# Decoder layer on one core: the gate and up products in plain fp32 on the weights as loaded, instead of three rounded products on split weights

## The reference

```python
def _L0_ffn_ref(x, w_gate, w_up, w_down):
    def _sparsify_2to4(h):
        B, S, I = h.shape
        g = h.reshape(B, S, I // 4, 4)
        a = jnp.abs(g)
        _, idx = jax.lax.top_k(a, 2)
        pos = jnp.arange(4)
        mask = (pos == idx[..., 0:1]) | (pos == idx[..., 1:2])
        return (g * mask.astype(g.dtype)).reshape(B, S, I)
    h = jax.nn.silu(jnp.einsum('bsh,hi->bsi', x, w_gate)) * jnp.einsum('bsh,hi->bsi', x, w_up)
    h_sparse = _sparsify_2to4(h)
    return jnp.einsum('bsi,ih->bsh', h_sparse, w_down)
...
x = x + _L0_attn_ref(_layernorm(x, axis=-1), ...)
x = x + _L0_xattn_ref(_layernorm(x, axis=-1), ctx_512, ...)
x = x + _L0_ffn_ref(_layernorm(x, axis=-1), L0_ffn_w_gate, L0_ffn_w_up, L0_ffn_w_down)
```

## Time and profile before

| | |
|---|---|
| time, median of 3 runs | 443.65 us (442.87 to 443.71) |
| time of the profiled execution | 448.27 us |
| its span | 446.5 us |
| PE busy | 394.7 us, 2912 matmuls |
| DVE busy | 286.2 us |
| ACT busy | 202.2 us |
| POOL busy | 159.9 us |
| mean granted clock of PE | 0.965 of 2.4 GHz |

### The profile page before, as it was taken

How to read it: one execution, slowest core, us unless ns; L and a number is a source line. 1 busy time by engine, 2 the same in 40 slices (tenths; PEclk the granted TensorE clock), 3 DMA queues, 4 the chain that set the end, 5 groups by cost and what they waited for, 6 DMA issues and landing times.

```text
span 446.5 us, 7877 instructions
## 1 busy us (share of the span) xinstructions
PE 394.7 (88%) x2912; PEld 320.3 (72%) x2912; DVE 286.2 (64%) x616; ACT 202.2 (45%) x524; POOL 159.9 (36%) x159
## 2 busy tenths in 40 slices
PE   4988899889899999869899999979899999577794
PEld 3767777667698777747698877857698877345783
DVE  3696931788769932748769961578769931344273
ACT  1422641477334741557444552287344551386230
POOL 4358730378310420356520340267520430155000
PEclk9996999999999999989999999999999999869698
DMA  7976300240001400240000510232000500210000
GB/s 239 373 253 206 95 25 23 73 119 19 2 0 54 143 23 25 72 124 12 2 1 7 166 25 1 70 112 51 0 1 0 167 24 24 84 36 1 1 0 23
DMA packets 34292, 29.93 MB, mean 67 GB/s; under 512 B 18512, under 2 KB 28880, under 8 KB 34000
## 3 DMA queue, kind: packets, MB, share of 16 engines
q1 hardware_dynamic: 34256, 29.44, 21.1%
HBM read 20.26 MB, written 5.24 MB: 57 GB/s over the span
## 4 chain that ended last, share of the span: by engine, by line
PE 64%; DVE 14%; DMA 7%; issue 5%; ACT 4%; SPq 3%; POOL 2%; POOLq 0%; DVEq 0%; ACTq 0%
PE ps L526 13%; PE ps L587 10%; PE ps L404 9%; PE ps L472 6%; PE ps L601 6%; DVE rope L728 4%; PE ps L435 4%; PE ps L512 3%; DMA q<-qx 3%; PE ps L490 3%; PE ps L412 2%; DMA prob<-in_masks 2%; POOL prob L934 2%; DVE total L759 2%; DVE mx L745 2%
## 5 line engine op out<-in xcount | busy, mean ns | idle before, releaser
L934 POOL TENSOR_TENSOR prob<-prob,inv 128x512 f32<-128x512 f32 x80 | 83.0, 1042 | 105.9 <-DVE inv L765 105.7
L404 PE MATMUL ps<-xnT,wqk_sb 128*128 128x256 f32 x320 | 79.1, 397 | 1.0 <-ACT xnT L989 0.7
L404 PEld LDWEIGHTS ps<-xnT,wqk_sb 128*128 128x128 f32 x320 | 61.5, 198 | 13.9 <-issue 4.9
L1026 ACT ACTIVATE prob<-ps,mx 128x128 f32<-128x128 f32 (+1 forms) x128 | 52.7, 431 | 13.7 <-DVE mx L743 11.6
L1036 ACT ACTIVATE pT<-ps 128x512 f32<-128x512 f32 x80 | 47.8, 601 | 18.6 <-PE ps L472 18.4
L728 DVE TENSOR_TENSOR rope<-ps,trig_sb 64x512 f32<-64x512 f32 x80 | 55.0, 688 | 1.1
L927 POOL TENSOR_TENSOR qs<-rope 128x512 f32<-128x512 f32 x32 | 40.9, 1278 | 37.6 <-DVE rope L728 37.6
L472 PE MATMUL ps<-ident_sb,prob 128*128 128x128 f32 x320 | 49.9, 281 | 4.5 <-POOL prob L934 4.2
L472 PEld LDWEIGHTS ps<-ident_sb,prob 128*128 128x128 f32 x320 | 37.7, 142 | 12.5 <-POOL prob L934 8.4
L743 DVE TENSOR_REDUCE mx<-ps 128x2 f32<-128x512 f32 (+1 forms) x48 | 33.1, 690 | 20.1 <-PE ps L454 19.7
L913 POOL TENSOR_TENSOR rstd<-vareps,power 128x1 f32<-128x1 f32 x24 | 13.1, 550 | 88.5 <-DVE vareps L707 88.3
(11 more groups left out here) (86 smaller groups left out, 677.7 us busy)
## 6 DMA issues: line engine op xcount, KB each, us to landing
k<-kx SPq DMA_DIRECT2D x32, 128.0 KB, 2.9
q<-qx SPq DMA_DIRECT2D x32, 128.0 KB, 2.6
vb<-v_sb SPq DMA_DIRECT2D x56, 64.0 KB, 2.1
wqk_sb<-in_wqk SPq DMA_DIRECT2D x4, 512.0 KB, 8.2
work<-in_wgu SPq DMA_DIRECT2D x4, 512.0 KB, 9.4
wo_sb<-in_wo SPq DMA_DIRECT2D x1, 2048.0 KB, 15.8
x_ln<-in_x SPq DMA_DIRECT2D x4, 256.0 KB, 2.8
x_res<-in_x SPq DMA_DIRECT2D x4, 256.0 KB, 3.0
```

What stands on the lines that cost most here:

```text
L404: mm = pe.matmul(o[:, half, :], wqk_sb[:, k, g, half, :], xnT[:, 0, k, :], start=(k == 0), stop=(k == KT - 1))
L934: pool.tensor_tensor(p, p, inv[:, i % ND, 0:g].unsqueeze(2).broadcast_to([P, g, 512 // g]), ALU.mult).then_inc(s_norm, 1)
L1026: ins = act.activation(prob[:, i % ND, h * k:(h + 1) * k], ps[:, BANK_S + i % 2, h * k:(h + 1) * k], ACT.Exp, bias=mx[:, i % ND, h:h + 1], ...
```

## The change

The weights stay as they are loaded, in one fp32 tensor `wgu_sb`, filled by one transfer that SP issues behind the value copies `v_blocks`, ahead of `wd_sb`. `round_weights` and `split_weights` are gone, with the waits on `s_wlo`. ACT copies the transposed residual once, in fp32, into `x3T`; DVE's subtraction is gone. `gate_up` makes four fp32 matmuls per bank in place of twelve rounded ones, 32 in place of 96 per batch. The split queries get two tensors of their own (`q2_hi`, `q2_lo`).

```diff
-        wgu_hi = sb("wgu_hi", [P, KT, 2, FC * 4, P], F32R)
-        wgu_lo = sb("wgu_lo", [P, KT, 2, FC * 4, P], F32R)
+        wgu_sb = sb("wgu_sb", [P, KT, 2, FC * 4, P])
...
-        x3_hi = sb("x3_hi", [P, KT, S], F32R)
-        x3_lo = sb("x3_lo", [P, KT, S], F32R)
-
-        q2p = [t[:].rearrange("p k s -> p (k s)").rearrange("p (t g n) -> p t g n", t=TT, g=HG)
-               for t in (x3_hi, x3_lo)]
+        x3T = sb("x3T", [P, KT, S])
+
+        q2p = [sb(f"q2_{part}", [P, TT, HG, P], F32R) for part in ("hi", "lo")]
...
                     wait_filled(sp, "down", b - 1)
-                else:
-                    sp.wait_ge(s_wlo, WCHUNKS)
...
-            for c in range(WCHUNKS // 2):
-                sp.dma_start(raw[:, 2 * c:2 * c + 2, :].rearrange("p c n -> p (c n)"),
-                             flat(wgu)[:, 2 * c * wcols:(2 * c + 2) * wcols]).then_inc(s_wraw[c], 16)
...
             v_blocks(None)
+            sp.dma_start(wgu_sb[:], wgu).then_inc(s_wgu, 16)
             sp.dma_start(wd_sb[:], wd).then_inc(s_wd, 16)
...
-                    by_hi = [(wp, x3_hi, k, m) for m in range(2) for k in range(KT) for wp in (wgu_hi, wgu_lo)]
-                    by_lo = [(wgu_hi, x3_lo, k, m) for m in range(2) for k in range(KT)]
-                    for n, (wp, xp, k, m) in enumerate(by_hi + by_lo):
-                        if xp is x3_lo and use == "gate00":
-                            wait_drained(pe, "ln3", b)
-
-                        mm = pe.matmul(half_banks(use, b)[:, m, :], wp[:, k, w, c * 4 + 2 * j + m, :],
-                                       xp[:, k, :], start=(n == 0), stop=(xp is x3_lo and k == KT - 1),
-                                       skip_group_check=True)
+                    for m in range(2):
+                        for k in range(KT):
+                            mm = pe.matmul(half_banks(use, b)[:, m, :], wgu_sb[:, k, w, c * 4 + 2 * j + m, :],
+                                           x3T[:, k, :], start=(k == 0), stop=(k == KT - 1))
                     mm.then_inc(filled(use, b), 1)
...
                 if b == 0:
-                    pe.wait_ge(s_wlo, WCHUNKS)
-                pe.wait_ge(s_x3hi, b + 1)
+                    pe.wait_ge(s_wgu, 16)
+                wait_drained(pe, "ln3", b)
...
-                dve.wait_ge(s_x3hi, b + 1)
-                dve.tensor_tensor(x3_lo[:], half_banks("ln3", b), x3_hi[:].bitcast(F32), ALU.subtract)\
-                   .then_inc(drained("ln3", b), 1)
...
-            def split_weights(c):
-
-                pool.wait_ge(s_whi, c + 1)
-                pool.tensor_tensor(lo_c[c], raw[:, c, :], hi_c[c].bitcast(F32), ALU.subtract)\
-                    .then_inc(s_wlo, 1)
...
-            def round_weights(c):
-
-                act.wait_ge(s_wraw[c // 2], 16)
-                act.activation(hi_c[c], raw[:, c, :], ACT.Copy).then_inc(s_whi, 1)
...
-                act.activation(x3_hi[:], half_banks("ln3", b), ACT.Copy).then_inc(s_x3hi, 1)
+                act.activation(x3T[:], half_banks("ln3", b), ACT.Copy).then_inc(drained("ln3", b), 1)
```

More of the change, by code:

```diff
@@ L47 @@
 XU = XU0 + XU1
-WCHUNKS = 8
-EARLY = 6
 UNITS = NQB + XU
@@ L125, in build @@
         rowmask_sb = sb("rowmask_sb", [P, HPT + 2])
-        wcols = KT * 2 * FC * 4 * P // WCHUNKS
         x_ln = sb("x_ln", [P, TT, D])
@@ L174, in build @@
         k4 = sb("k4", [P, HPT // 2, 2, HG, S], F32R)
-        raw = work[:].rearrange("p (c k) s -> p c (k s)", c=WCHUNKS)
         hidden = work[:, 0:4 * FC, :].rearrange("p (c j) s -> p c j s", c=FC)
@@ L208, in build @@
         s_vb = sem("s_vb")
[L209 to L212, removed]
+        s_wgu = sem("s_wgu")
         s_score = sem("s_score")
@@ L275, in free_ring @@
                 eng.wait_ge(s_sums, n - 2)
-        flat = lambda w: w.rearrange("p k w c n -> p (k w c n)")
-        hi_c = [flat(wgu_hi[:])[:, c * wcols:(c + 1) * wcols] for c in range(WCHUNKS)]
-        lo_c = [flat(wgu_lo[:])[:, c * wcols:(c + 1) * wcols] for c in range(WCHUNKS)]
         block = es.enter_context(nc.Block())
@@ L948, in batch @@
                     unit_norm(b, i)
-                    if b == 0 and i < WCHUNKS - EARLY:
-                        split_weights(EARLY + i)
                 if more:
@@ L979, in _ @@
                 rope_sums(f"q{g}", None, GROUPS + g + 1)
-            for c in range(EARLY):
-                split_weights(c)
             for b in range(B):
@@ L1132, in _ @@
                 keys(t, t + 1)
-            for c in range(WCHUNKS):
-                round_weights(c)
             act.wait_ge(s_zero, 2)
```

## The result

| | before | after |
|---|---|---|
| median of the runs, us | 443.26 (441.71 to 443.71, 4 runs) | 451.70 (449.58 to 453.57, 4 runs) |
| the profiled execution, us (its span) | 448.27 (446.5) | 452.08 (450.1) |
| ratio after / before | | 1.0164, 95% interval 1.0110 to 1.0218 |

The changed kernel is slower, by 1.6% in the ratio; the two medians by themselves are 1.9% apart. The forecast of 434.6 us was wrong in sign.

What follows compares the result with a forecast made beforehand. PE was taken to set the pace up to the first comparison of the FFN, DVE behind it. Three middle batches gave 7.0 us, the last 2.1, the start 0: 9.1 us off the median, 434.6 us, range 433 to 436.5.

Steps and rivals of the forecast that it cites:

- The products: Gate and up matmuls on PE: 32 fp32 at 0.216 us, 6.90 us per batch in place of 11.63, 4.73 less.
- The bound, from L601: Check on the fp32 matmul's price: L601, with other operands, has 3.46 / 16, the same; nothing of that shape runs slower.
- The page that was set aside: Skill page on fp32: four passes, priced at 0.484 us per matmul, 15.5 us per batch; the trace's 0.216 was preferred.
- An fp32 matmul is dearer here than at L404: Rival, 4%: at 0.484 us per matmul, the 16th ends 1.9 us later than now in a middle batch; together 452 us.
- A middle batch: FFN of three batches: comparisons start 2.32 us earlier, DVE sets the pace behind them; 3 x 2.32 = 7.0 us saved.
- The last batch: Last FFN, PE partly at half clock: the 16th matmul ends 2.1 us earlier, last `down` left at 5.42; 2.1 us saved.
- The start: Work before the first FFN: removed preparation on POOL and ACT and the later weight load are worth 0, ±0.5 us.
- The clock rivals: Clock falls in a middle batch's new PE wait (12%, 437.5 us); the last `down` gets the full clock (15%, 432.6 us).
- the second of these rivals: Rival, 15%: after a new PE pause before the last batch's first `down`, the last `down` gets full clock; 432.6 us.

Runs made afterwards that it cites:

- four_rounded: The kernel before with a fourth rounded product added (low weights by low activations), 128 matmuls per batch; 454.90 us, ratio 1.0228.
- bf16_corrections: The kernel before with its three products kept, the two that hold a low part made from bf16 operands; 443.38 us, ratio 0.9981.
- fp32_last: The kernel before with fp32 products on the rounded operands, low parts left out, in the last batch alone; 444.26 us, ratio 1.0006.
- rounded_once: The kernel before with only the high parts multiplied and all work that made the low parts removed; 426.47 us, ratio 0.9603.
- one_rounded: The kernel before with one rounded product in place of three, all preparation of the low parts kept; 431.00 us, ratio 0.9708.
- two_rounded: The kernel before without the product with the activations' low part, eight rounded matmuls per bank instead of twelve, preparation kept; 437.09 us, ratio 0.9836.
- fp32_chunk1: The kernel before with fp32 products on the rounded operands, low parts left out, in the FFN's second chunk alone; 447.14 us, ratio 1.0071.
- fp32_chunk0: The kernel before with fp32 products on the rounded operands, low parts left out, in the FFN's first chunk alone; 448.58 us, ratio 1.0088.
- fp32_products: The kernel before with four fp32 products per bank on the rounded operands, all preparation and the early weight load kept; 450.20 us, ratio 1.0139.
- early_load: The changed kernel with the gate and up weights' transfer back at its old place, ahead of wo_sb; 449.94 us, ratio 1.0132 to the kernel before.

## Why the prediction was wrong

The products of a batch on PE and the period, from the chains of waits above. Where a row there doesn't hold the whole batch, the first number is records times 0.121, an estimate from four_rounded's row; for the kernels marked * the period is taken from ACT's copies into `x3_hi`. For bf16_corrections the first number is 11.65 less the 0.5 us that the starts show. The periods are the first two (of the kernel before the second alone, by the earlier trace rows; fp32_last, whose first three batches are the same, has 99.8 twice).

| kernel | products of a batch, us | period, us | median, us |
|---|---|---|---|
| rounded_once * | 3.9 | 96.5 to 96.6 | 426.5 |
| one_rounded * | 3.9 | 97.1 to 97.3 | 431.0 |
| two_rounded | 7.7 | 97.9 | 437.1 |
| bf16_corrections | 11.2 | 99.5 | 443.4 |
| before | 11.65 | 99.7 | 443.3 |
| fp32_chunk1 | 12.87 | 100.7 | 447.1 |
| fp32_chunk0 | 12.85 | 101.0 | 448.6 |
| fp32_products | 14.08 | 101.6 to 101.9 | 450.2 |
| after | 14.08 | 101.8 to 101.95 | 451.7 |
| four_rounded | 15.45 | 103.3 | 454.9 |

**"The products" is the step that failed.** It said "16 of L404 take 3.45 us in a row, 0.216 each". The 3.45 us are right and the count is not: they are 16 records, and the program issues 8 matmuls there (two groups of `rope_group`, four to a group, as the text on the kernel says). An fp32 product costs 3.45 / 8 = 0.431 us, and three rounded ones cost 0.363. The place to see it was in the earlier trace rows: x320 for L404, where the program has 160 such matmuls. (The 2912 matmuls of the table of the kernel before are records in the same way.) The bound, from L601, was miscounted in the same way, so it excluded nothing. A `down` stands as x16; in the code it is a loop over four `j` and two `t`, 8 matmuls. The text on the kernel, which lets each of the last four instructions of `sparsify` release four matmuls of `down`, counts records there: it is two.

**The page that was set aside fits.** The Trainium skill ("FP8 and Floating Point Precision", section "TensorE Precision Notes") says that true fp32 takes four passes. The prediction priced a pass at a rounded product and got 0.484, and then dismissed it by the row. Over this case's rows the matmul costs 0.431 in a run of L404 and 0.439 in the stage, and four rounded products 4 x 0.1206 = 0.482 (four_rounded). So the trace agrees with four passes that are somewhat shorter each, 0.108 to 0.110 us, than a rounded matmul by itself. That each record stands for two passes is argued from these durations and was not shown.

**The rival that happened** was "An fp32 matmul is dearer here than at L404" (4%). Its break-even of 0.37 us lies between the measured 0.363 of three rounded products and 0.439, so its sign follows. Its name was wrong: the matmul costs here what it costs at L404. Its time, 452 us, came out near 451.7 with two errors against each other. The price was too high (0.484 for 0.439), and the charge was the comparisons' delay alone. By that charge the measured delay of 8.57 - 7.37 = 1.20 us would cost three batches 3.6 us; the three periods grew by 2.1, 2.24 and 2.67.

**"A middle batch" was right in one direction.** It said that PE sets the pace up to the first comparison and DVE behind it. When PE gets shorter, that holds: two_rounded saves 3.9 us on PE, moves the comparison by 1.92 and the period by 1.8. When PE gets longer it does not: 2.43 us more on PE (14.08 against 11.65) cost 2.1 and 2.24 in the first two periods (and 2.67 in the third, with the clock mixed in), chunk 1 costs most of what chunk 0 does, and PE is full from the first product to 157. The kernel before stands at the bend: its own chain runs over PE up to 146.54, and DVE has no gap there. Above it a microsecond of PE costs 0.8 to 1.1 us of the period, below it 0.5 and, from two products to one, 0.2. The prediction read PE's 0.7 us of slack in the earlier trace rows and did not ask what 2.4 us more would do with it.

**"The last batch"** was to be 2.1 us shorter and is 1.4 longer in the profiles. The first half of its products takes 9.74 us against 8.24, 1.5 more, which fits the dearer product: in both the clock rises some 5.1 us after the first of them (granted clock 0.50 in 422 to 424 and 0.96 in 424 to 426 in the changed kernel). The last `down` was left at 5.42 and took 5.27. How much the batch costs over many executions stays open: fp32_last can't be told from the kernel before.

**"The start" at 0, with half a microsecond of play, was right.** The first product comes 0.47 us earlier. The value copies that the earlier place of the load had held up take 10.74 us to issue instead of 17.61, as the prediction thought possible, and nobody waited for them: the first normalisation on POOL moves from 44.57 in fp32_products, behind six subtractions, to 44.29.

```profile
19.21 10.74 SPq L281 DMA_DIRECT2D vb<-v_sb  x16
...
44.29 1.04 POOL L907 TENSOR_TENSOR prob<-prob,inv 128x512 f32<-128x512 f32 x1 [7.04 <-DVE inv L741]
```

early_load and fp32_products say the same with their times. So all the removed preparation was covered by other work, and the one visible term was the one that had the wrong sign.

**The clock rivals.** There is no new wait on PE in a middle batch, since PE is what is late, and so nothing for the clock to fall behind. The pause ahead of the first `down` of the last batch, on which the second of these rivals rested, did not come either: the products run up to it. The last `down` at full clock didn't come in the profiled execution (5.27 us), but it did in that of fp32_products, with the same products: `down` there takes 3.73 us, and its execution of 450.34 us is 1.7 shorter than the 452.08 of the changed kernel. 1.5 us of that difference is this piece.

```profile
441.49 3.73 PE ps L609 x16
```

## What to carry to other kernels

Before a duration is taken from a row of a trace, set its count against the number of instructions that the program issues: one fp32 matmul left two records here, and a price per record was wrong by two. A rule that contradicts a row is a reason to count that row again, and not a thing for the row to overrule. Where two engines are both nearly full, a change has to be costed with another slope in each direction: what makes the fuller engine longer counts at once, and what makes it shorter counts only until the other one takes over.

## What the hardware showed

- A plain fp32 matmul (128x128 weights, 256 columns) costs 0.431 to 0.440 us in a stream at full clock and shows as two records of MATMUL and two of the weight load. A `float32r` one costs 0.12 and shows as one.
- bf16 operands save a little over `float32r` at this shape: 0.114 us a product in a stream that is two thirds bf16, against 0.12 for one that is all `float32r`.
- The clock at the end isn't set by the length of the wait alone. The last `down` waits 2.46 us in the changed kernel and takes 5.27, with a granted clock of 0.50 in 442 to 444; in fp32_last it waits 2.45 and takes 3.73, with 1.00 from 434 to 438. Over the kernels it took 3.73, 5.2 to 5.4, or 6.73 us, so two profiled executions can differ by 3 us in this place, whatever the change. The five kernels in which it waited 3.3 us all had the half clock there; of the six with a wait of 2.2 to 2.5 us, two had. The two rows:

```profile
441.50 5.25 PE L577 MATMUL ps<-wd_sb,work 128*128 128x256 f32 x16 [2.46 <-DVE work L773]
```

```profile
434.71 3.72 PE L609 MATMUL ps<-wd_sb,work 128*128 128x256 f32 x16 [2.45 <-DVE work L805]
```

What decides between these levels was not settled.
